# Two loads ahead of a packed transpose, the second quarter of low x behind a maximum, and the third quarter of y ahead of two high halves

## The reference

```python
deg = clip(adj.sum(axis=1), 1.0);  dis = deg ** -0.5
diffusion = (dis[:, None] * adj * dis[None, :]) @ x - x
norms = maximum(norm(x, axis=-1), 1e-8)
sim = x @ x.T / (norms[:, None] * norms[None, :])
attn = softmax(beta * sim * adj, axis=1)
x = layernorm(x + diffusion + sigmoid(alpha) * (attn @ x - x))
x = layernorm(x + relu(adj @ (x @ weights)))
```

## Time and profile before

| what | value |
|---|---|
| median of 3 runs | 658.79 us (658.75 to 659.19) |
| the profiled execution | 658.59 us |
| its span, first to last instruction | 656.7 us |
| PE busy | 638.0 us, 97% |
| DVE busy | 517.8 us, 79% |
| ACT busy | 412.2 us, 63% |
| POOL busy | 236.8 us, 36% |
| granted TensorE clock, mean | 0.998 |

### The profile page before, as it was taken

The page is one execution under the profiler, slowest core; times in us unless marked ns, Lnnn a source line. Parts: engine busy times, 40 slices in busy tenths (PEclk is TensorE's granted clock), DMA queues, the critical chain, the costliest instruction groups (busy, mean ns, idle before and its releaser), DMA issues.

```text
span 656.7 us, 16155 instructions
## 1 busy us (share of the span) xinstructions
PE 638.0 (97%) x5087; PEld 463.5 (71%) x5087; DVE 517.8 (79%) x1565; ACT 412.2 (63%) x768; POOL 236.8 (36%) x249
## 2 busy tenths in 40 slices
PE   7788999999999999999999999999999999999996
PEld 6456777777777777777777777888888864444465
DVE  4987999999999999999999998878777773334443
ACT  6998999999999999999999998612111110000000
POOL 5998553553554554544544546400000000000000
PEclk9999999999999999999999999999999999999999
DMA  7878999999999999999999996300000000000000
GB/s 282 303 161 215 278 272 239 279 256 253 280 267 239 285 263 233 285 263 242 292 258 240 307 237 97 77 1 1 0 0 0 0 0 1 16 17 16 16 33 33
DMA packets 165019, 107.36 MB, mean 163 GB/s; under 512 B 144384, under 2 KB 148608, under 8 KB 164992
## 3 DMA queue, kind: packets, MB, share of 16 engines
q1 hardware_dynamic: 164992, 107.04, 61.6%
HBM read 69.27 MB, written 2.10 MB: 109 GB/s over the span
## 4 chain that ended last, share of the span: by engine, by line
PE 86%; DVE 4%; DMA 4%; ACT 2%; issue 2%; POOL 1%; DVEq 0%; SPq 0%; POOLq 0%; ACTq 0%
PE ps_s L1005 22%; PE ps_s L1198 17%; PE ps_e L1170 15%; PE ps_e L1016 8%; PE ps_e L1038 8%; PE ps_acc L1038 7%; PE ps_e L1041 4%; PE ps_acc L1041 4%; DMA eTx<-e_parts 2%; DVE scores L708 1%; DMA x_keep<-in_x 1%; PE ps_e L1054 1%; DVE e_parts L729 1%; PE ps_acc L1182 1%; PE ps_s L1054 1%
## 5 line engine op out<-in xcount | busy, mean ns | idle before, releaser
L1005 PE MATMUL ps_s<-xn_parts,xn_signed 128*128 128x512 f16 x756 | 203.3, 379 | 4.2 <-DVE cmax L708 4.2
L708 DVE CUSTOM_DVE_ANT_1 scores<-ps_s,adj_bytes 128x512 f32<-128x512 f32 x252 | 171.6, 683 | 24.4 <-PE ps_s L1005 15.2
L523 ACT ACTIVATE scores<-scores,col 128x1024 f32<-128x1024 f32 x128 | 157.4, 1232 | 2.1 <-DVE col L719 1.9
L482 ACT ACTIVATE adj_bytes<-land 128x1024 uint8<-128x1024 f32 x128 | 133.5, 1047 | 0.6 <-POOL packed L343 0.6
L351 POOL TENSOR_SCALAR e_parts<-scores 128x1024 f16<-128x1024 f32 x64 | 68.5, 1071 | 157.7 <-ACT scores L523 154.2
L1170 PE MATMUL ps_e<-y_parts,stage 128*128 128x256 f16 x896 | 98.0, 273 | 0.0
L1005 PEld LDWEIGHTS ps_s<-xn_parts,xn_signed 128*128 128x128 f16 x756 | 68.4, 98 | 40.2 <-DVE cmax L708 4.3
L1170 PEld LDWEIGHTS ps_e<-y_parts,stage 128*128 128x128 fp8e4 x896 | 87.7, 98 | 10.1
L530 ACT ACTIVATE eT_parts<-ps_e 128x512 f16<-128x512 f32 x128 | 75.8, 595 | 28.7 <-PE ps_e L1016 27.9
L723 DVE SCALAR_TENSOR_TENSOR eT_parts<-ps_e,eT_parts 128x512 f16<-128x512 f32 x128 | 87.4, 683 | 1.9 <-ACT eT_parts L530 1.9
L729 DVE SCALAR_TENSOR_TENSOR e_parts<-scores,e_parts 128x1024 f16<-128x1024 f32 x64 | 88.4, 1382 | 0.4 <-POOL e_parts L351 0.4
(11 more groups left out here) (128 smaller groups left out, 967.1 us busy)
## 6 DMA issues: line engine op xcount, KB each, us to landing
land<-in_adj SPq DMA_DIRECT2D x128, 512.0 KB, 5.4
x_keep<-in_x SPq DMA_DIRECT2D x4, 512.0 KB, 5.6
out<-u SPq DMA_DIRECT2D x7, 256.0 KB, 2.1
eTx<-e_parts SPq DMA_TRANSPOSE x64, 4.3
packT<-packed SPq DMA_TRANSPOSE x16, 6.5
out<-u SPq DMA_DIRECT2D x2, 128.0 KB, 1.7
scores<-in_L_gnn_weights SPq DMA_DIRECT2D x1, 64.0 KB, 2.0
col<-in_L_gnn_beta SPq DMA_DIRECT2D x1, 0.5 KB, 7.1
```

Source lines behind the costliest of these rows:

```text
L482: nc.scalar.activation(adj_bytes[:, q, i * CH:(i + 1) * CH], land[:, q, i, :], ACT.Copy, scale=float(BYTE_TOP[q] >> i), accum_out=deg[:, i ...
L523: nc.scalar.activation(piece, piece, ACT.Exp, bias=neg_max[q], scale=abs_beta, accum_out=csum[:, q, i:i + 1]).then_inc(exp_done, 1)
L708: nc.vector.tensor_tensor_reduce(scores[:, q, o:o + BANK].rearrange("p (k q) -> p k q", k=K), score_bank(h, r == 0 if start else False).re ...
L1005: ins = nc.tensor.matmul(score_bank(h, start), xn_signed[:, q, part, :], xn_parts[:, other, o:o + BANK], start=(part == 0 and other == 0), ...
```

## The change

It reorders instructions on each engine; no instruction is added or taken away. The diff:

```diff
-    LATE_ATTEND = (0, 4, 5, 1, 6, 7, 2, 3)
+    LATE_ATTEND = (0, 4, 5, 1, 2, 6, 7, 3)
# SP
             turn_ex(0, 0, 1)
             turn_ex(1, 1, 0)
+            def row_4(i):
+                sp.wait_ge(cast_done, 2 * C + i + 1)
+                land_piece(1, 0, i)
+            row_4(0)
+            row_4(1)
             turn_adj(0, 0)
+            turn_ex(1, 1, 1)
+            row_4(2)
+            row_4(3)
+            turn_ex(2, 0, 0)
-            for k in range(G):
+            for k in range(1, G):
                 turn(1, k)
# POOL, end
             y_rows(0)
             y_rows(1)
+            y_rows(2)
             ex_high(R - 1, 1, 0, place=1)
             ex_high(R - 1, 1, 1, place=1)
-            y_rows(2)
             y_rows(3)
# ACT, start
             norm_root(0)
+            norm_root(1)
             squares(2)
-            norm_root(1)
...
             cast(2, 0, 0)
+            exps(1, 1, 2)
             cast(2, 0, 1)
-            exps(1, 1, 2)
# DVE, start
             row_max(0, 0)
-            mask(1, 1, 0, start=True)
-            mask(1, 1, 1, start=True)
-            x_low(1)
+            for h in range(4):
+                mask(1, 1, h, start=True)
             e_low(0, 0)
-            mask(1, 1, 2, start=True)
-            mask(1, 1, 3, start=True)
+            mask(1, 1, 4, start=True)
             e_low(0, 1)
             ex_low(0, 0, 0)
-            mask(1, 1, 4, start=True)
             mask(1, 1, 5, start=True)
             ex_low(0, 0, 1)
-            e_low(0, 2)
             mask(1, 1, 6, start=True)
             mask(1, 1, 7, start=True)
             row_max(1, 1)
+            e_low(0, 2)
+            mask(2, 0, 0)
             e_low(0, 3)
-            mask(2, 0, 0)
+            x_low(1)
             mask(2, 0, 1)
# DVE, end
             e_low(R - 1, 0)
-            ex_low(R - 1, 1, 0)
             e_low(R - 1, 1)
             y_low(1)
+            ex_low(R - 1, 1, 0)
             ex_low(R - 1, 1, 1)
# PE, start: the new order
             cosines(1, 1, 0), (1, 1, 1), (1, 1, 2)
             turn_e(0, 0, 0), turn_e(0, 0, 1)
             cosines(1, 1, 3), (1, 1, 4), (1, 1, 5)
             first_attend(0)
             cosines(1, 1, 6)
             first_attend(1)
             turn_e(0, 0, 2), turn_e(0, 0, 3)
             cosines(1, 1, 7), (2, 0, 0), (2, 0, 1)
             first_attend(2), first_attend(3)
             cosines(2, 0, 2)
             first_attend(4)
             cosines(2, 0, 3)
```

More of the change, by code:

```diff
@@ L1095, in _ @@
             cosines(1, 1, 1)
+            cosines(1, 1, 2)
             turn_e(0, 0, 0, True, FIRST_EXP)
             turn_e(0, 0, 1, True, FIRST_EXP)
-            cosines(1, 1, 2)
             cosines(1, 1, 3)
             cosines(1, 1, 4)
+            cosines(1, 1, 5)
             first_attend(0)
-            cosines(1, 1, 5)
+            cosines(1, 1, 6)
             first_attend(1)
@@ L1105, in _ @@
             turn_e(0, 0, 3, True, FIRST_EXP)
-            cosines(1, 1, 6)
             cosines(1, 1, 7)
+            cosines(2, 0, 0)
+            cosines(2, 0, 1)
             first_attend(2)
-            cosines(2, 0, 0)
             first_attend(3)
-            cosines(2, 0, 1)
+            cosines(2, 0, 2)
             first_attend(4)
-            cosines(2, 0, 2)
             cosines(2, 0, 3)
```

## The result

The median of six executions is **665.32 us** (662.54 to 666.83), against 659.08 us for the kernel before beside them (six executions, 658.75 to 660.36): a ratio of 1.0086 with the interval 1.0061 to 1.0110. The change makes the kernel slower by some 5.7 us, where 2.6 were forecast, and the time lies above the range. The six executions fall into two groups: three at a mean granted clock of 0.993 take 665.84 to 666.83 us, three at 0.996 or 0.997 take 662.54 to 664.79. The profiled execution is of the first group: 666.83 us with a span of 664.9, 8.2 us more than the span of before, at a mean granted clock of 0.993 instead of 0.998.

What follows compares the result with a forecast made beforehand. The prediction took POOL's own list to bound the start and the landing of the last transpose the end. It summed 658.59 + 1.3 (start) + 1.3 (end), SP and head at 0, to 661.2 us, range 657.3 to 662.4.

Steps and rivals of the forecast that it cites:

- The bound of the start: Up to PE's wait ending at 60.09 us: POOL decides; PE's cosines at 61.4, PE itself ready at 60.95; +1.3 us.
- POOL's own list: POOL's instructions from 27.9 to 58.8 us, without idle time: whatever lengthens them is paid in full.
- Masks first: DVE's start: mask (1,1,4) waits for the third cast, 29.5 to 31.05; the maximum comes only 0.45 us forward, at 37.0.
- `x_low` later: Start, behind row block 1's maximum: waits for L364, PE idle some 4 us, POOL loses a full 1.1 us.
- PE held by a chain of its own on top: +2.3: Upper bound of the start's loss, beside the +1.3 us taken.
- SP: 0: SP's two loads ahead of packed transpose and turn_ex(1, 1, 1): it lands by 57.7 to 58.5, when PE comes; 0.
- Rival C: Slower still: turn_ex(1, 1, 1) lands after PE needs it, or PE's wait for x_low runs on; +1, 662.3; chance 0.07.
- The head: 0: norm_root(1) ahead of squares(2): free, covered by ACT's wait for x's fourth quarter; otherwise at most 0.2 us.
- The end: End of the attention part: last transpose sets it, landing at 426.7 instead of 425.38 behind y_rows(3) and late low halves; +1.3 us.
- The gain of `LATE_ATTEND`: End, PE's 0.61 us wait for piece 6: ready piece 2 fills it, piece 3 waits; PE gains 0.33 of it.
- Rival A: End: DVE keeps the port, ex_low follows y_low(1) at once; last transpose at 424.8 to 424.95; 659.4 in all; chance 0.20.
- The sum: Profiled execution: 658.59 + 1.3 for the start + 1.3 for the end = 661.2 us; chance 0.46.

Runs made afterwards that it cites:

- start_only: The kernel before with only the start's new order on DVE, PE and ACT, without the norm_root and SP edits: 662.86 us beside 659.17, ratio 1.0060.
- after: The whole change, as in its profiled execution: 666.83 us; median of six executions 665.32 us beside 659.08 of the kernel before, ratio 1.0086.
- after_again: The whole change once more, unaltered, against the kernel before on the same chip: 664.94 us beside 659.45, ratio 1.0085.
- after_fill: The whole change plus 11 float32 matmuls ahead of first_attend(2), results unread: 662.24 us beside 659.44 of the kernel before, ratio 1.0045.
- sp_only: The kernel before with only SP's new order, two loads ahead of the packed transpose and turn_ex(1, 1, 1): 659.69 us beside 659.17, ratio 1.0006.
- norm_only: The kernel before with only norm_root(1) moved ahead of squares(2): 659.87 us beside 659.17, ratio 1.0008.
- end_only: The kernel before with only the end's edits (LATE_ATTEND, y_rows(2) ahead of the high halves, ex_low(31,1,0) behind y_low(1)): 659.97 us beside 659.17, ratio 1.0014.
- start_old_late: The start's new order with x_low(1) at its old place, plus the new LATE_ATTEND: 659.26 us beside 659.44 of the kernel before, ratio 0.9990.
- start_xlow_old: The kernel before with the start's new order, but x_low(1) kept behind mask (1,1,1): 658.88 us beside 659.28, ratio 0.9994.
- end_late_dve: The kernel before with the new LATE_ATTEND and the end's new order on DVE alone: 660.50 us beside 659.44, ratio 1.0016.
- end_late_pool: The kernel before with the new LATE_ATTEND and the end's new order on POOL alone: 658.53 us beside 659.44, ratio 0.9981.
- after_no_sp: The whole change with SP's queue as before: 663.88 us beside 659.45 of the kernel before, ratio 1.0063.
- after_no_norm: The whole change with norm_root(1) back behind squares(2): 665.29 us beside 659.45 of the kernel before, ratio 1.0084.
- start_fill: The kernel before with the start's new order plus 11 float32 matmuls ahead of first_attend(2), results unread: 660.88 us beside 659.28, ratio 1.0025.

## Why the prediction was wrong

**The bound of the start** was half right. POOL's last `minus_x` still ends last and PE waits for it by the same 1.2 us as before. But I wrote that the start is bound by "POOL's own list", and left PE only 0.45 us of distance (60.95 against 61.4). POOL isn't alone: its high halves hang on exponentials, these on maxima, these on PE's scores. The trace of before had a sign of it, in its chain of waits:
```profile
53.12 0.20 ACT scores L523
53.34 0.14 POOL e_parts L351
```
POOL's high half of 53.33 follows the end of its exponential (53.32) at once, so ACT had no time in hand there. I took a row without an idle time in brackets for a row that nobody holds up. With PE's path this close, any further delay of PE becomes the bound, and it did: POOL waits 2.79 us for the exponential in start_only. (The 9.54 of 10 us that I gave for POOL's busy time is that of 20 to 30 us; from 50 to 60 us it is 9.50, so nothing hangs on it.)

**Masks first** came as forecast. Mask 4 waits 1.40 us for the third cast (1.55 forecast). The maximum of row block 1 stands 11.84 us behind that of row block 0 in after, and 12.28 in before: 0.44 less, where 0.45 was forecast. Only this is one of two courses: in start_only and after_again it stands at 13.3. The two DMA low halves of row block 0 on DVE, in start_only:
```profile
31.97 1.79 DVE L729 SCALAR_TENSOR_TENSOR e_parts<-scores,e_parts 128x1024 f16<-128x1024 f32 x1
...
34.30 2.11 DVE L729 SCALAR_TENSOR_TENSOR e_parts<-scores,e_parts 128x1024 f16<-128x1024 f32 x1
```
In after each takes 1.22 us: there DVE has the port first, here POOL. I had 0.2 us for such collisions; they can be 1.5. No time of a timed execution can be laid to the one or the other, so its share in the medians stays open.

**`x_low` later** is the step that failed. Its mechanics were right: it waits for L364, takes 2.64 us (2.75 forecast), lengthens POOL's next high half to 1.90 us (0.9 more; 1.1 forecast), and PE stands for 3.96 (some 4 forecast). Measured from the maximum of row block 0, PE goes on at 16.76 us, where the forecast had 16.74 (41.5 less 24.76). The next step failed: PE was to reach its first turn of row block 1 at 44.8, 20.04 us behind that maximum, and does at 21.69. What is missing is a price behind the wait: in the 3.4 us that begin 1 us behind it the granted clock is 0.50 and PE's matmuls take about twice as long. With the wait filled, after_fill reaches the turn at 20.04 us, as forecast. The fillers show the low clock to be worth 1.7 us in the traces, 2.0 and 2.7 in the medians. With PE only 0.45 us from being the bound, this makes PE the bound of the start, by way of the scores, the maximum and the exponentials that POOL waits for.

A trace of before could not show this for the start, as its waits there were 1.34 us at most and the clock stayed at 1.00; but a wait of 4 us, three times as long as any of them, was no case for reckoning PE's path at the old speed, and my upper bound, "PE held by a chain of its own on top: +2.3", took no account of a slower PE. The Trainium skill (TensorE: Matmul & The Clock Gate, Part 1) says that a monitor sets the clock by how busy PE has lately been, and puts the penalty of the ramp at under 1% of a typical kernel span. The trace agrees with the first, by the low clock behind the wait; the price here, 1.7 to 2.7 of 659 us, is under 1% as well, but 1% would be 6.6 us, more than all that was at stake. With the price found here it would have been a rival of its own: start +3.0 to +4.0, the whole 662.9 to 663.9.

**SP: 0** was wrong by 1.1 us. I judged the later transpose by when PE needs its result, and it was in time for that. The one who waited was POOL, for the transpose to have read its source. A DMA has two who wait for it, the reader of its destination and the next writer of its source, and I priced only one. It was nearly hidden: sp_only shows the same order at no cost, and it took the late `x_low` to bring it out. Rival C named both of the mishaps (the transpose behind two loads, a wait for `x_low` that runs on) and was given 0.07 and +1.0 us together, too little of either.

**The head: 0** can't be told from what was measured (norm_only +0.7 us, interval -0.1 to +1.2). But the sum for the profiled execution had no term for a low clock in the head, which costs 1.7 us in an execution that has it; the profiled execution of before had none, that of after had.

**The end** had the right mechanism at a price too high, +1.3 for 0.75 in the profile and 0.8 in the median of end_only. Step by step from the start of `y_low(0)`: the first low half ends 9.3 us later (forecast 9.5), the second transpose lands 16.2 us later (forecast 16.8), before 15.5. Half of the 0.6 us is the moment at which the first transpose lands, the other half is the spacing of the two:
```profile
431.18 0.28 PE L1047 MATMUL ps_e<-x_parts,eTx 128*128 128x256 f16 x1 [1.17 <-DMA eTx<-e_parts]
...
433.68 0.28 PE L1047 MATMUL ps_e<-x_parts,eTx 128*128 128x256 f16 x1 [1.01 <-DMA eTx<-e_parts]
```
PE (timeline of after) meets them 2.5 us apart and not 2.8. The gain of `LATE_ATTEND` can't be seen: start_old_late has it and start_xlow_old hasn't, and their ends are 0.0 and -0.1. Rival A, by which DVE keeps the port, is out: in after, end_only and end_late_dve alike the pair of low halves takes 4.05 us, with the last of `y_rows(3)` in it. The Trainium skill (SBUF — State Buffer, Who interferes with whom) says that issue order decides who blocks; the trace agrees, with 2.85 us for the low half that was issued behind `y_rows(3)`, and 1.15 us for the last one of end_late_pool, beside which POOL has nothing left.

**The sum.** Forecast 1.3 (start) + 0 (SP) + 1.3 (end) = 2.6. Found in the traces: 1.6 for the start's order, 1.7 for the clock, 1.1 for SP, 0.8 for the end, in sum 5.2, which is what after_again shows (4.4 + 0.8); after itself took the other course at the maximum of row block 1 and shows 4.3. The medians have 5.7, since half of the executions of after have the lower mean clock, and only a quarter of those of before in the table. The two terms that I had priced above 0 were right within half a microsecond; the loss of 3 us and the miss of the range are the clock, for which I had no term, and SP, whose term I had put at 0.

## What to carry to other kernels

A wait on TensorE of 3 to 4 us that a reorder newly opens is to be priced twice, as a wait and as a stretch at half the clock around its end (here 3.4 us of it, worth about 1.7), even where the engine seemed to have room; the cheap test is to fill it with matmuls whose result nobody reads. Before medians that differ by a few tenths of a per cent are compared, sort the executions by their mean granted clock: a low stretch that comes in some and not in others was worth 1.7 us here, more than most of the edits. Before a DMA is put behind other transfers, look at both ends of it: who reads its destination, and who wants to write its source next. Where two engines share a port and two transfers follow from their work, the first of the two transfers counts as well as the last: delaying the first one cost 1.4 us in the profile (1.0016) though the second was ready no later, and moving one POOL instruction out from ahead of the low halves gained 0.7 to 0.9 us in the profiles of three kernels.

## What the runs showed of the hardware that I had not expected

- The granted clock fell to 0.50 for 3.4 us, beginning between 0.1 us ahead and 1.0 us behind the end of waits of PE of 3.40 to 3.96 us (after, after_again, start_only, after_no_sp); in after_no_norm it had fallen at 38.9 already, 4.2 us ahead of the end of the wait, and came back at 45.7.
- The length of the last wait alone doesn't tell when it falls. It stayed at 1.00 in the start of before, with waits of at most 1.34 us, and in start_fill behind waits of 1.92 and 0.95 us. But in the head of norm_only it fell at 16.4 us, behind a wait of 1.10 us, and stayed at 1.00 behind one of 1.09 us at the same place in before.
- A low stretch in the head costs 1.7 us up to the maximum of row block 0: 10.06 to 10.10 us in eight profiled executions, 8.41 to 8.43 in twelve.
- The same instruction lists take one of two courses in different executions: the maximum of row block 1 comes 11.84 us behind that of row block 0 in after and 13.30 in after_again. Who gets the shared port first differs from one execution to the next and is worth 1.5 us there.
- A transpose that lands 4.3 us after its issue in the quiet end takes 6.25 us when issued behind two loads of 512 KB and a packed transpose; which of these holds it was not separated.
